# A gated recurrence with a routed feed-forward layer: the order and the widths of the TensorE products in the front of the kernel

## The reference

```python
# branch s: a gated scan over time (state of 64)
x_norm = layernorm(xn, ln_in_g, ln_in_b)
x_norm = x_norm + conv3(x_norm) + conv_b              # depthwise, 3 taps along time
gate, input_gate = split(x_norm @ gate_w.T + gate_b)
Bm = x_norm * sigmoid(input_gate) @ B_w.T + B_b       # the "drive" of each step
Cm = x_norm @ C_w.T + C_b
A_bar = expm(dt_A * A)                                # 64 x 64
for t: state = layernorm(state @ A_bar + Bm[t], ln_st_g, ln_st_b)
s = ((Cm * states) @ D_w.T + D_b) * sigmoid(gate)
# branch g: 8 experts, 2 of them for each token
y = layernorm(xn) * ln_gamma + ln_beta
abel = gelu(y @ abel_w + abel_b)
top2, weights = softmax(top_k(y @ moe_gate_w + moe_gate_b, 2))     # the "router"
moe = sum over top2 of weights * (gelu(y @ ew1[e] + eb1[e]) @ ew2[e] + eb2[e])
for i in range(3): moe = moe @ expm(gens[i])          # 128 x 128 each
mixed = a sigmoid-gated mix of abel and moe
out = x + s * silu(y_residual + mixed)
```

## Time and profile before

| | |
|---|---|
| median of 3 runs | 389.48 us (387.97 to 390.64) |
| the profiled execution's own time | 385.57 us |
| its span, first to last instruction | 383.7 us |
| PE busy, DVE busy, ACT busy, POOL busy | 324.5, 272.3, 194.8, 165.5 us |
| first scan step on PE (L1145) | at 96.81 us |
| first transposes of a tile (L1579) | at 134.10 us |

### The profile page before, as it was taken

How to read it: one execution, slowest core, us unless ns; L and a number is a source line. 1 busy time by engine, 2 the same in 40 slices (tenths; PEclk the granted TensorE clock), 3 DMA queues, 4 the chain that set the end, 5 groups by cost and what they waited for, 6 DMA issues and landing times.

```text
span 383.7 us, 11682 instructions
## 1 busy us (share of the span) xinstructions
PE 324.5 (85%) x4034; PEld 249.2 (65%) x4046; DVE 272.3 (71%) x1301; ACT 194.8 (51%) x581; POOL 165.5 (43%) x239
## 2 busy tenths in 40 slices
PE   1799999969888699889989998898999897877870
PEld 0688877769455468666777886776767645655440
DVE  5874766484778668668766665679899755888872
ACT  1159731513233246466656677468776628664210
POOL 7930000027777776777777555334555500000000
PEclk9999655988999969999999999889999989999696
DMA  7499930001151337657657768946565232000002
GB/s 263 127 242 185 176 46 0 2 7 49 47 202 58 95 105 225 211 189 261 223 197 253 240 215 261 321 138 224 199 222 193 71 125 108 29 28 29 33 26 87
DMA packets 44158, 54.81 MB, mean 143 GB/s; under 512 B 6840, under 2 KB 28767, under 8 KB 44095
## 3 DMA queue, kind: packets, MB, share of 16 engines
q1 hardware_dynamic: 37743, 42.51, 37.8%
q0 software_dynamic: 4544, 9.39, 7.6%
q10 hardware_dynamic: 1808, 2.10, 1.7%
HBM read 14.15 MB, written 16.63 MB: 80 GB/s over the span
## 4 chain that ended last, share of the span: by engine, by line
PE 33%; DVE 10%; issue 3%; ACT 3%; DMA 2%; SPq 1%; DVEq 0%; POOL 0%; ACTq 0%
PE bank L1145 8%; PE bank L1586 7%; PE bank L1596 6%; PE bank L1485 2%; PE bank L1616 2%; PE bank L1571 2%; DVE wT L1044 2%; PE bank L1579 1%; DMA token_rows<-rows_out,token_rows_i 1%; DMA pulls<-token_rows 1%; DVE xT L1492 1%; DVE late L1058 1%; DVE xT L1497 1%; DVE sqj L1030 1%; ACT xpad L1404 1%
## 5 line engine op out<-in xcount | busy, mean ns | idle before, releaser
L1821 POOL DMA_INDIRECT token_rows<-rows_out,token_rows_i x78 | 75.6, 969 | 59.5 <-ACT rows_out L1718 24.2
L1145 PE MATMUL bank<-Mrep,wT 32*32 32x64 f32 x2368 | 65.4, 226 | 16.2 <-DVE wT L1044 15.9
L1145 PEld LDWEIGHTS bank<-Mrep,wT 32*32 32x32 f32 x2368 | 41.7, 107 | 54.3 <-issue 52.4
L1807 POOL DMA_INDIRECT sorted_rows<-late,slots x64 | 62.0, 968 | 19.7 <-issue 13.7
L1711 ACT ACTIVATE desk<-bank,record 128x128 f32<-128x128 f32 x156 | 49.1, 367 | 36.8 <-PE bank L1586 35.1
L1586 PE MATMUL bank<-desk,record 128*128 128x128 f32 x312 | 57.8, 310 | 0.0
L1058 DVE SCALAR_TENSOR_TENSOR ring<-bank,Rho,Dv 128x64 f32<-128x64 f32 x112 | 31.6, 283 | 29.6 <-PE bank L1145 27.1
L1596 PE MATMUL bank<-record,desk 128*128 128x129 f32 x312 | 49.4, 282 | 0.0
L1586 PEld LDWEIGHTS bank<-desk,record 128*128 128x128 f32 x312 | 42.5, 197 | 7.5 <-issue 0.7
L1596 PEld LDWEIGHTS bank<-record,desk 128*128 128x128 f32 x312 | 42.4, 197 | 0.1
L1703 ACT ACTIVATE desk<-bank,cols 128x128 f32<-128x128 f32 x78 | 36.1, 463 | 4.0 <-PE bank L1579 4.0
(11 more groups left out here) (337 smaller groups left out, 660.1 us busy)
## 6 DMA issues: line engine op xcount, KB each, us to landing
record<-experts SPq DMA_DIRECT2D x78, 290.5 KB
sorted_rows<-zero_rows SPq DMA_DIRECT2D x2, 2515.5 KB, 28.7
desk<-sorted_rows SPq DMA_DIRECT2D x26, 193.5 KB
pulls<-token_rows SPq DMA_DIRECT2D x8, 516.0 KB, 5.4
X<-in_L_attn_x ACTq DMA_DIRECT2D x4, 512.0 KB, 6.0
out<-xT SPq DMA_DIRECT2D x8, 256.0 KB, 2.0
token_rows<-rows_out,token_rows_i POOLq DMA_INDIRECT x78
experts<-in_L_ffn_ew SPq DMA_DIRECT2D x1, 1024.0 KB, 9.6
```

The lines of the kernel that those rows point to most:

```text
L1145: t = pe.matmul(psY[q], wT[q, 32 * c:32 * c + 32], Mrep[q, c, :], start=(c == 0), stop=(c == 1))
L1807: pool.indirect_dma_start(sorted_rows[h], bass.IndirectOffsetOnAxis(ap=slots[:, j, q:q + 1], axis=0), sort_rows[:, q, :], None)\
L1821: pool.indirect_dma_start(token_rows[h], bass.IndirectOffsetOnAxis(ap=token_rows_i[:, g:g + 1], axis=0), rows_out[:, g % OUT_PLACES, :], N ...
```

## The change

In words:

- `router` now moves 128 columns instead of 8: `router_wide` is `router_w` with 120 columns of zeros, and each group's product writes over the zeros of the one before. `B_product` moves 128 columns (zeros and `B_wT`) for seven of its eight products, from the last to the first. The sum of the drives takes two steps in one product of 128 columns, four products instead of eight, and `first_start` adds the halves with one more VectorE instruction.
- `warm(14)` stands ahead of everything on TensorE and `warm(8)` ahead of the series: products of the identity with itself into bank 3, whose results nobody reads.
- In the series the four identity products of 128 columns become one of 512, which stands ahead of the wait for the term before.
- The ew2 transposes move up by two terms (and use three banks in turn), z's by none, with one more tile within the series; four of the eight routers stand within the series, terms 6 to 9, and the others between the squarings of A.
- Both copies of A's squares are ScalarE's (`A_copies`). The convolution's first four centre taps are VectorE's and the last four ScalarE's (before, they took turns).
- `scan_bias` and what follows from it move from before the gens' squarings to behind the counts; on VectorE the statistics of A's rows and the copies of the biases move likewise, behind the routing and behind the slots. `B_product(0)` stands behind the last squaring. Two rotations instead of four stand before `B_product(2)`.
- The 1 MB load of ew2 goes from the end of SyncE's list to ScalarE's queue, behind the four loads of x. On GpSimd the bias parts are written once instead of four times, the copy to `ident_gc` stands behind them, and two memsets of the zero columns come in.

```diff
-        B_wT = sb("B_wT", [P, S])
+        B_wide = sb("B_wT", [P, 2 * S])
+        B_wT = B_wide[:, S:2 * S]
...
-        router_w = sb("router_w", [P, E])
+        router_wide = sb("router_w", [P, P])
+        router_w = router_wide[:, 0:E]
...
-            load(ew2, I["L0_ffn_ew2"].rearrange("e (k p) d -> p e k d", p=P), "ew2_loaded")
...
+            pool.memset(router_wide[:, E:P], 0.0)
+            pool.memset(B_wide[:, 0:S], 0.0)
...
-            for i in range(2):
-                t = pool.tensor_tensor(bias3[:, i], bias_mix[:, i, :].unsqueeze(1).broadcast_to([3, SUB, P]),
-                                       bias_rest[:, 0, i, :].unsqueeze(1).broadcast_to([3, SUB, P]), ALU.add)
-            t.then_inc(sem("bias3_ready"), 1)
+            pool.tensor_tensor(bias3, bias_mix[:, :, :], bias_rest[:, 0], ALU.add).then_inc(sem("bias3_ready"), 1)
+            pool.tensor_copy(ident_gc[:, 0:P], ident[:, :])
...
-        DVE_CENTRED = range(0, NB, 2)
+        DVE_CENTRED = NB // 2
...
-                for k in range(8):
+                for k in range(7, -1, -1):
                     x = gi[:, 2 * g + k // 4, (k % 4) * P:(k % 4 + 1) * P]
-                    t = pe.matmul(B_bank(i)[:, k * S:(k + 1) * S], x, B_wT[:, :], start=True, stop=True)
+                    wide = min(k, 1)
+                    t = pe.matmul(B_bank(i)[:, (k - wide) * S:(k + 1) * S], x, B_wide[:, (1 - wide) * S:2 * S], start=True, stop=True)
...
-                    t = pe.matmul(banks[6][:, q * E:(q + 1) * E], x, router_w[:, :], start=True, stop=True)
+                    t = pe.matmul(banks[6][:, q * E:q * E + P], x, router_wide[:, :], start=True, stop=True)
...
-                pe.wait_ge(sem("A_squared_T"), k + 1)
-                if k:
-                    pe.wait_ge(sem("A_squared"), k)
+                pe.wait_ge(sem("A_squared"), 2 * k + 1)
                 half = slice(0, S)
...
+            def warm(times):
+                for _ in range(times):
+                    pe.matmul(banks[3][:, 0:P], ident[:, :], ident[:, :], start=True, stop=True)
+
+            pe.wait_ge(sem("ident_ready"), 2)
+            warm(14)
             pe.wait_ge(sem("expm_loaded"), 48)
-            pe.wait_ge(sem("ident_ready"), 2)
...
+            warm(8)
...
+                pe.matmul(o[:, :], whole_idents[:, 0, :], whole_idents[:, k - 1, :].unsqueeze(1).broadcast_to([P, 4, P]), start=True, stop=False)
+                if i:
+                    pe.wait_ge(sem("taylor"), i)
                 for m in range(4):
-                    pe.matmul(o[:, m * P:(m + 1) * P], whole_idents[:, 0, :], whole_idents[:, k - 1, :], start=True, stop=False)
-                    if m == 0 and i:
-                        pe.wait_ge(sem("taylor"), i)
-                    t = pe.matmul(o[:, m * P:(m + 1) * P], XT[:, m, :], EX[:, m, :] if i else ident[:, :], start=False, stop=True)
+                    t = pe.matmul(o[:, m * P:(m + 1) * P], XT[:, m, :], EX[:, m, :] if i else ident[:, :], start=False, stop=(m == 3))
...
-                elif i >= 4 and i < TAYLOR - 1:
+                    ew2_transposes(0)
+                elif i >= 4:
                     z_transposes(i - 4)
-                    if i >= 5:
-                        ew2_transposes(i - 5)
+                    if i <= 6:
+                        ew2_transposes(i - 3)
+                    if i >= 6:
+                        router(i - 6)
             pe.wait_ge(sem("taylor"), TAYLOR)
             for m in range(4):
                 t = pe.transpose(banks[1][:, m * P:(m + 1) * P], EX[:, m, :], ident[:, :])
             t.then_inc(sem("exp_T"), 1)
-            z_transposes(5)
+            z_transposes(6)
+            router(4)
             square_A(0)
-            z_transposes(6)
-            router(0)
+            z_transposes(7)
+            router(5)
             square_A(1)
-            z_transposes(7)
-            router(1)
-            router(2)
+            router(6)
+            gate_in(0)
             square_A(2)
-            router(3)
-            gate_in(0)
+            router(7)
+            gate_in(1)
...
-            gate_in(1)
+            gate_in(2)
             square_A(4)
...
+            gate_in(3)
+            square_gens(0)
+            gate_in(4)
+            square_gens(1)
+            gate_in(5)
+            square_gens(2)
+            gate_in(6)
+            square_gens(3)
+            gate_in(7)
+            square_gens(4)
+            B_product(0)
+            pe.wait_ge(sem("counted"), 1)
+            pe.wait_ge(sem("logits_read"), 1)
+            pe.matmul(banks[6][:, 256:256 + 2 * HALVES * E], earlier[:, :], places[:, :, :, Q - 1:NS:Q], start=True, stop=True)
+            pe.matmul(banks[6][:, 288:288 + 2 * HALVES * E], ones[:, :], places[:, :, :, Q - 1:NS:Q], start=True, stop=True).then_inc(sem("count_sums"), 1)
...
+            for k in range(8, 16, 2):
+                t = pe.matmul(banks[3][:, 0:2 * S], ones[:, :], Dv[:, k:k + 2, :].rearrange("p k n -> p (k n)"), start=(k == 8), stop=(k == 14))
             t.then_inc(sem("drive_sum"), 1)
-            for e in range(4):
-                ew2_rotation(e)
+            ew2_rotation(0)
+            ew2_rotation(1)
             B_product(2)
-            for e in range(4, E):
+            for e in range(2, E):
                 ew2_rotation(e)
...
+
+            act.dma_start(ew2, I["L0_ffn_ew2"].rearrange("e (k p) d -> p e k d", p=P)).then_inc(sem("ew2_loaded"), 16)
...
-            def A_copy(k):
-                act.wait_ge(sem("A_square_T"), k + 1)
-                act.copy(ET[0:S, 3, 0:S], banks[1][0:S, 0:S]).then_inc(sem("A_squared_T"), 1)
+            def A_copies(k):
+                act.wait_ge(sem("A_square"), k + 1)
+                act.copy(EX[0:S, 3, 0:S], banks[2][0:S, 0:S]).then_inc(sem("A_squared"), 1)
+                act.copy(ET[0:S, 3, 0:S], banks[1][0:S, 0:S]).then_inc(sem("A_squared"), 1)
...
-            series(4)
-            for i in range(5, TAYLOR):
-                affine(i - 5)
+            for i in range(4, TAYLOR):
                 series(i)
-                normed(i - 5)
-                if i < TAYLOR - 1:
-                    ew2_copy(i - 5)
+                if i < 8:
+                    ew2_copy(i - 4)
+                affine(i - 4)
+                normed(i - 4)
+            act.wait_ge(sem("exp_T"), 1)
+            act.copy(ET[:, :, :], banks[1][:, :].rearrange("p (m n) -> p m n", m=4)).then_inc(sem("A_squared"), 1)
+            act.wait_ge(sem("half_columns"), 1)
+            affine(6)
+            normed(6)
+            A_copies(0)
+            conv_centre(4)
+            affine(7)
+            conv_centre(5)
+            normed(7)
+            A_copies(1)
+            conv_centre(6)
+            conv_centre(7)
+            A_copies(2)
             act.wait_ge(sem("rows_copied_a"), 1)
             act.mul(half_gc_b, bcast[:, 2 * P + E:2 * P + E + 1], 0.5)
...
             act.activation(junk_col[:, :], eps_col[:, :], ACT.Gelu)
             act.wait_ge(sem("bias3_ready"), 1)
             gate(0)
+            A_copies(3)
             gate(1)
+            A_copies(4)
             gate(2)
...
-                if i in DVE_CENTRED:
+                if i < DVE_CENTRED:
                     dve.wait_ge(sem("affine"), n + 1)
...
@@ -849,33 +848,10 @@
             dve.tensor_scalar(B_wT[:, :], B_wT[:, :], row_mean_b, 0.5, ALU.subtract, ALU.mult).then_inc(sem("B_centred"), 1)
             dve.wait_ge(sem("half_columns"), 1)
             conv_before(0)
...
+                conv_before(i)
+                conv_after(i - 1)
+            conv_after(NB - 1)
 
...
+            dve.tensor_scalar(AbC[:, :], EX[0:S, 3, 0:S], row_mean[0:S], None, ALU.subtract).then_inc(sem("scan_matrix"), 1)
             gated(4)
-            dve.wait_ge(sem("scan_bias"), 1)
-            dve.tensor_copy(bias_all[:, 0:2, :], banks[7][:, 0:2 * S].rearrange("p (c n) -> p c n", c=2)).then_inc(sem("scan_biases"), 1)
-            dve.tensor_copy(Mrep[:, :, :], banks[7][:, 2 * S:4 * S].rearrange("p (c n) -> p c n", c=2))
-            dve.wait_ge(sem("scan_biases"), 1)
-            dve.tensor_tensor(bias_all[:, 2, :], bias_all[:, 0, :], bias_all[:, 1, :], ALU.add).then_inc(sem("scan_biases"), 1)
+            dve.wait_ge(sem("scan_matrix"), 1)
+            dve.tensor_scalar(Mx[:, :], AbC[:, :], col["ln_st_g"][0:S], None, ALU.mult).then_inc(sem("scan_matrix"), 1)
             dve.wait_ge(sem("count_sums"), 1)
             sums = banks[6][:, 256:256 + 2 * HALVES * E].rearrange("p (e j h) -> p h e j", h=HALVES, j=2)
...
+            dve.wait_ge(sem("scan_bias"), 1)
+            dve.tensor_copy(bias_all[:, 0:2, :], banks[7][:, 0:2 * S].rearrange("p (c n) -> p c n", c=2)).then_inc(sem("scan_biases"), 1)
+            dve.tensor_copy(Mrep[:, :, :], banks[7][:, 2 * S:4 * S].rearrange("p (c n) -> p c n", c=2))
+            dve.wait_ge(sem("scan_biases"), 1)
```

(3 more changed lines are left out.)

114 lines of the change are left out of this document (25 added, 89 removed).

## The result

The changed kernel takes 377.68 us, the median of four runs (376.69 to 383.99), and the kernel before 389.14 on the same chip (387.97 to 390.64): the ratio is 0.9695, with a 95% interval of 0.9645 to 0.9745. That is 11.5 us less, or 11.9 by the ratio. The forecast was 15.7 less, 373.8.

The account below looks back on a forecast made before the run. Two chains behind the front, scan steps and GpSimd's scatters, bound the time, with TensorE's clock at half speed in the front. Slots 16.9 us and steps 14.7 earlier give 15.7 together: 389.5 - 15.7 = 373.8 us, range 369 to 383.

Parts of the forecast that it names:

- the forecast case: Whole kernel: high clock from the first term, one cold stretch behind the drive sum; 373.8 us, chance 0.56.
- rival 2: Series runs cold: the first four terms cost 3.05 us each instead of 1.9, + 4.6: 378.4 us; chance 0.15.
- The low clock behind the drive sum: TensorE between slots and first step: clock lost while idling, 5.2 us at half speed, costing 2.6 us.
- the near absence of a wait for rows: First tile of the loop: scatters start 16.9 us earlier, steps 14.7, so the tile's 0.96 us wait goes.
- case 2: Same as rival 2: the series runs at the low clock, 378.4 us; chance 0.15.
- The terms of the series: Front: four products 1.05 us, tail 0.2, copy 0.60, semaphores 0.05; 1.9 us a term at 2.4 GHz.
- VectorE's additions beside GpSimd: Statistics in the front: additions slowed to 1.29 us by two bias instructions; one short instruction instead takes 2 us off VectorE.
- rival 6: The loop doesn't follow: scatters or loads hold the first tiles, half the gain is lost; 382 us, chance 0.06.
- rivals 3 and 5: 3: clock falls behind the series, 380.8 us, chance 0.13. 5: wide products don't hold the clock, 394 us, chance 0.04.
- Copies 0 to 3: ScalarE's first copies of the series, behind TensorE's terms: they start at 12.3, 14.2, 16.1 and 18.5 us.
- rival 4: Loads at the start: ew2 delays biases and matrices by up to 3.0 us; 375.3 to 376.8 us, chance 0.06.
- First steps and slots: End of the front: slots 16.9 us earlier (66.1), first step 14.7 earlier (82.1), together 15.7 us of gain.

Follow-up runs that it names:

- e8: The kernel before with only the router's products made 128 columns wide; 381.27 us, ratio 0.9753.
- e1: The changed kernel with ew2's load back in SyncE's list, behind abel_w; 371.48 us, ratio 0.9505.
- e2: The changed kernel with ew2's load last on ScalarE's queue, behind its nine small loads; 371.55 us, ratio 0.9518.
- e5: e2 without warm(14) and warm(8); 369.88 us, ratio 0.9454.
- the first profile of before: Profiled execution of the unchanged kernel before, from which the prediction took its rows; 385.57 us.
- the second one: The kernel before profiled a second time, unchanged; its profiled execution took 388.44 us, with a span of 386.6.
- e6: e2 with 11 filler products of the identity before the wait for the drive sum and 6 before the rotations; 370.48 us, ratio 0.9475.
- e10: e2 with TensorE's two counts products moved from behind B_product(0) to ahead of square_gens(3); 364.80 us, ratio 0.9388.
- e7: e2 with router, B products and drive sum narrow again, as before the change; 369.83 us, ratio 0.9498.
- e3: The changed kernel with the router's products 8 columns wide again; 379.85 us, ratio 0.9752.
- e4: The changed kernel without warm(14) and warm(8); 375.91 us, no ratio given.

## Why the prediction was right, and where it failed

The time is inside the stated range, 377.7 instead of 373.8, and part of the forecast's mechanism came as told. But it is outside the forecast case's own range (370 to 377) and nearer to rival 2's 378.4, and of the signs that the prediction had named most failed: the clock was low until 31.3 us, the copies of the series started 1.8, 2.8 and 3.4 us apart, square_gens began at 55, the slots were there at 73, the first step came at 88.6. The low clock behind the drive sum and the near absence of a wait for rows came. A low clock in the series was what it had said would make it wrong by case 2.

**What held.** The long cold stretch went (1.00 from 32 to 72 us), and e8 shows that widening the router does it alone. The terms of the series run 1.85 us apart when ScalarE is there (e1, e2: 12.45, 14.30, 16.14), as priced (1.9). The squarings keep their pace of 2.56. VectorE's additions beside GpSimd went from 1.29 us to 0.31. Each of the steps behind the series came late by nearly the same amount: tanh 51.80 for 45.0, the convolution's end 52.7 for 45.7, square_gens(0) 54.98 for 47.9, the cast's end 73.17 for 66.1, the drive sum 74.47 for 67.45. So the sums from one to the next were right to 0.3 us (the prediction names five instructions on z tiles in ScalarE's list where six stand, but its 8.4 us for the list are near the 8.2 that it took). The cold stretch behind the drive sum came where it was forecast, for 6.8 us. The 5.2 that the prediction took from before was a window and not the stretch, which runs from 82.8 to 89.6 there, 6.8 us as well. The rows kept up with the first tile (a wait of 0.28), so the loop followed: rival 6 didn't come, nor rivals 3 and 5.

**The step that failed** is "Copies 0 to 3 then start at 12.3, 14.2, 16.1 and, with half a microsecond of small matrices, 18.5". It lets the first copy wait for TensorE alone. Of the moved load it had counted the bytes (rival 4: SyncE's loads delayed by up to 3.0 us), but not the issues that stand behind it on ScalarE, which the copy stands behind in turn. The first copy started at 15.37, 3.1 late. The wait that this gave TensorE cost its clock, so the terms ran cold, as in rival 2, but for another reason: it wasn't that the terms are too short of work to warm it (in e5, without warming products, the second term is fast); the clock was high and was lost. The series took 26.3 us from the first copy to the last where 22.4 were forecast, 3.9 more. 3.1 and 3.9 are the 7.0 by which everything behind was late. e2 takes both back: its series takes 20.2 us from the first copy to the last, so that the forecast's 22.4 were too many even for a warm series; its cast (64.28) comes earlier than the forecast's 65.9, its first step (79.02 for 82.1) too, and its time is 371.55.

With these 7.0 the gain comes out at 8.7 us, just what the first tile moved by, and the time at 380.8; the runs have a gain of 11.5. All sums start from the first profile of before, a short execution. By the second one, nearer the median, the first tile moved by 10.4. The last microsecond stays open; it is within the spread of the runs. That the measured time lies only 3.9 above the forecast, and not 7.0, is luck in part: the profile that all sums start from was a short one, so that the runs gained more than its rows tell.

**Rival 4** had the right load and the wrong way. Its traffic did delay some of SyncE's loads, by up to 1.9 us (`D_w`), but none that was waited for; x and the matrices came as early as without it. A row that could have warned of the queue was in the trace of before: SyncE's two issues of the zero fill, 2.5 MB each, held their engine for 15.70 us.

```profile
16.67 15.70 SPq L284 DMA_DIRECT2D sorted_rows<-zero_rows  x2
```

**First steps and slots.** The forecast moved both and took 15.7 as one number between them. e6 and e10 show that they aren't alike: 1.8 us of the step alone gave no measurable gain, 5.0 us of the cast, with 6.2 of the step, gave 5.1.

## What to carry to other kernels

When a load is moved onto a compute engine's queue, look at what is issued behind it: an issue that had to wait held its engine here, and the chain behind lost more than the wait (3.1 us of delay and 3.9 of slower products). Small loads first, the big one last, cost nothing here. Warming products bought 0.7 us of the chain here where the work behind them came in time, and were lost where it didn't. And before shortening a chain, see which of two meets later at the join: the wait there (0.28 to 2.35 us for the tile's rows, none in e7) tells which one it is, and VectorE's idle row ahead of the counts showed the 5 us that were to be had.

## What was not expected of the hardware

- An issue of one column of 128 values on ScalarE took 5.58 us behind four loads of x and one of 1 MB, and 0.63 us behind the four of x alone. e3 and e4, with the same queue as the changed kernel, repeat it (5.59 and 5.61). SyncE was held too in the changed kernel, for 14.33 us by the two issues of the zero fill behind 1 MB of expert weights. What an issue waits for, no trace here shows.

```profile
14.60 14.33 SPq L285 DMA_DIRECT2D sorted_rows<-zero_rows  x2
```

- The granted clock doesn't tell everything at the start. The window from 12 to 17.6 us of e4 reads 1.00, and the same eight records take 1.91 us at 11.48 and 2.08 at 16.18, against 1.05 at 22.39. In that first stretch it is the pace of the products, not PEclk, that shows at which speed TensorE runs.

```profile
12.00:17.60 5.60, 3.23 (x14) 2.54 (x14) 3.70 (x18) 1.97 (x3) 4.96 (x15) 1.00 1.15 145
```

- Busy isn't enough: 22.50 of 22.50 us busy went at 0.50, half of them with narrow routers and the rest with gate products, small squarings and biases; with wide routers the same stretch, 20.85 of 22.50 us busy, went at 1.00 (e8). Nor was it in the changed kernel: 13.35 of 13.60 us busy at 0.50, from 17.6 on, without one narrow router.
